# State space stage of a six-stage transformer kernel: its first chunk's normalisation, input projections, gates and step sizes made inside cross attention's last batches

## What is computed

```python
def _L0_attn_ref(u, in_proj_w, dt_projs_weight, dt_projs_bias, x_proj_w, A, D, ...):
    xz = u @ in_proj_w.T
    x, z = jnp.split(xz, 2, axis=-1)
    x = jax.nn.silu(x)
    dt = jax.nn.softplus(x @ dt_projs_weight.T + dt_projs_bias)
    BCp = (x @ x_proj_w.T).reshape(Bsz, L, NHEADS, -1)
    ...
    x_sum = xh.sum(axis=-1)
    zt = Ac[None, None] * (0.5 * dt)[..., None]
    abar = (1.0 + zt) / (1.0 - zt)
    u_in = Bc * ((dt * x_sum)[..., None] / (1.0 - zt))
    # h = abar * h + u_in, step by step; y = Re(C h) summed, times the gate silu(z), projected out

x = x + _L0_xattn_ref(_layernorm(x, axis=-1), ctx_1024, ...)
x = x + _L0_attn_ref(_layernorm(x, axis=-1), ...)
```

## Time and profile before

| what | value |
|---|---|
| median of 3 runs | 1026.29 us (1025.15 to 1029.08) |
| the profiled execution's own time | 1024.24 us |
| its span, first to last instruction | 1022.5 us |
| PE busy | 823.2 us (81%) |
| DVE busy | 746.9 us (73%) |
| ACT busy | 562.1 us (55%) |
| POOL busy | 204.5 us (20%) |
| cross attention | from 0 to 251.1 us of the span |
| state space stage, up to the first step of its recurrence | 252.2 to 299.2 us |

### The profile page before, as it was taken

The page is one execution under the profiler, slowest core; times in us unless marked ns, Lnnn a source line. Parts: engine busy times, 40 slices in busy tenths (PEclk is TensorE's granted clock), DMA queues, the critical chain, the costliest instruction groups (busy, mean ns, idle before and its releaser), DMA issues. The chain is left out here.

```text
span 1022.5 us, 26783 instructions
## 1 busy us (share of the span) xinstructions
PE 823.2 (81%) x9567; PEld 490.9 (48%) x9567; DVE 746.9 (73%) x2473; ACT 562.1 (55%) x1398; POOL 204.5 (20%) x217
## 2 busy tenths in 40 slices
PE   5899999995975788696663397896986999999686
PEld 2577777774322233242131275563664555555343
DVE  5688888884389999999996795456463667767757
ACT  3788898886675658575240476453343333333244
POOL 1467766663000000000000011002210000000136
PEclk9999999998897788898797598997897999999889
DMA  7111111100000000000000903100570000000001
GB/s 241 33 44 43 40 37 41 41 6 2 1 0 0 1 1 0 1 1 0 1 0 8 166 2 117 52 5 19 205 274 1 1 1 0 0 0 1 1 11 31
DMA packets 23157, 36.54 MB, mean 36 GB/s; under 512 B 5668, under 2 KB 19748, under 8 KB 20644
## 3 DMA queue, kind: packets, MB, share of 16 engines
q1 hardware_dynamic: 23080, 35.53, 11.6%
HBM read 34.48 MB, written 1.05 MB: 35 GB/s over the span
## 5 line engine op out<-in xcount | busy, mean ns | idle before, releaser
L381 ACT ACTIVATE xa_prob<-xa_s,xa_nmax 128x257 f32<-128x257 f32 x256 | 128.1, 503 | 21.6 <-DVE xa_nmax L466 19.8
L568 POOL TENSOR_TENSOR xa_prob<-xa_prob,xa_rinv 128x1028 f32<-128x1028 f32 x64 | 121.5, 1900 | 75.8 <-DVE xa_rinv L473 74.6
L466 DVE CUSTOM_DVE_ANT_0 xa_s<-xa_s_ps,xa_nbias 128x257 f32<-128x257 f32 x256 | 93.2, 420 | 12.3 <-ACT xa_prob L381 6.4
L1492 POOL TENSOR_TENSOR mo_disp_t<-mo_disp_t,mo_rst 128x256 f32<-128x256 f32 x16 | 9.9, 616 | 377.0 <-DVE mo_rst L1472 377.0
L2117 PEld LDWEIGHTS ca_z_ps<-ca_xn_t,ca_m_t 128*128 128x128 f32 x512 | 62.0, 198 | 30.5 <-issue 26.0
L2200 ACT COPY ca_z<-ca_z_ps 128x512 f32<-128x512 f32 x64 | 37.5, 585 | 69.0 <-PE ca_z_ps L2117 69.0
L242 PE MATMUL xa_t_ps<-identity,xa_prob 128*128 128x128 f32 x512 | 69.4, 279 | 3.7 <-ACT xa_p_t L390 2.1
L2117 PE MATMUL ca_z_ps<-ca_xn_t,ca_m_t 128*128 128x128 f32 x512 | 67.9, 288 | 4.1 <-ACT ca_xn_t L2194 3.9
L456 DVE COPY xa_kvs<-xa_kv_ps 128x512 f32<-128x512 f32 x64 | 44.1, 689 | 34.5 <-PE xa_kv_ps L216 34.5
L242 PEld LDWEIGHTS xa_t_ps<-identity,xa_prob 128*128 128x128 f32 x512 | 54.8, 141 | 25.3 <-issue 25.3
L390 ACT COPY xa_p_t<-xa_t_ps 128x1024 f32<-128x1024 f32 x64 | 63.4, 990 | 2.7 <-PE xa_t_ps L242 2.7
(11 more groups left out here) (327 smaller groups left out, 1929.1 us busy)
## 6 DMA issues: line engine op xcount, KB each, us to landing
xa_ctx_t<-in_ctx_t SPq DMA_DIRECT2D x64, 128.5 KB, 2.1
room<-in_ctx_t SPq DMA_DIRECT2D x8, 1028.0 KB, 6.6
room<-in_ctx_n SPq DMA_DIRECT2D x8, 1024.0 KB, 4.8
ss_wx<-in_ss_wx SPq DMA_DIRECT2D x1, 2048.0 KB, 7.8
xres<-in_x SPq DMA_DIRECT2D x4, 256.0 KB, 5.5
out_x<-xres SPq DMA_DIRECT2D x4, 256.0 KB, 2.3
ma_mask_u<-in_mask SPq DMA_DIRECT2D x4, 128.5 KB
room<-in_ca_wk SPq DMA_DIRECT2D x1, 512.0 KB, 4.9
```

What stands on the lines that cost most here:

```text
L381: nc.scalar.activation(prob[:, r, g, :], s_sb[:, b, g, :], ACT.Exp, bias=nmax[:, r, g:g + 1], scale=-1.0, accum_out=rsum[:, r, g:g + 1]).t ...
L466: nc.vector.tensor_tensor_reduce(out=s_sb[:, b, g, :], in0=s_ps[:, g, 0:S], in1=nbias[:, g, :], scale=1.0, scalar=3e38, op0=ALU.add, op1=A ...
L568: nc.gpsimd.tensor_tensor(prob[:, r, :, :], prob[:, r, :, :], bc(rinv[:, r, :].rearrange("p (g o) -> p g o", o=1), (P, G, S)), ALU.mult).t ...
```

## The change

Everything of chunk 0 up to `tx` (the product of step size and input sum) moves from the beginning of the state space block into the slots of tiles 14 and 15 of cross attention and the three slots behind them. The tiles and semaphores it needs are made ahead of both stages, in the new class `FirstChunk`. PSUM is borrowed: `kv_ps` for the transpose and the fourth projection, `s_ps[0]` to `s_ps[2]` for the first three, `s_ps[0]` and `s_ps[1]` again for the sums of the step sizes. The statistics of tiles 0 to 3 give `rstd` and `nmr` through Ln and Exp instead of Sqrt and a reciprocal, so cross attention's Exp now comes from the set that has Ln too (L413 before). Silu is loaded between the turns of batches 61 and 62, and the Exp and Ln set again before softplus. The state space block then computes `rstd` and `nmr` of all 16 tiles in the same manner and starts with the projection of B.

```diff
+            def chunk_turn():
+                pe.wait_ge(ch.xn_ready, QT)
+                pe.wait_ge(kv_ready, NT)
+                for i in range(QT):
+                    last = nc.tensor.transpose(kv_ps[:, i * P:i * P + P], ch.xn[:, i, :], ident[:, :])
+                last.then_inc(ch.xnt_mm, 1)
+
+            def chunk_in(parts):
+                pe.wait_ge(ch.xnt_ready, 1)
+                pe.wait_ge(ss_ld, SS_LD)
+                pe.wait_ge(s_ready, G * NT)
+                for j in parts:
+                    nc.tensor.matmul(s_ps[:, j, :] if j < 3 else kv_ps[:, :], ss_in[:, j * P:j * P + P], ch.xnt[:, :],
+                                     start=True, stop=True).then_inc(ch.in_mm, 1)
+
+            def chunk_sizes(part):
+                pe.wait_ge(ch.in_ready, 2)
+                for kb in range(2):
+                    last = nc.tensor.matmul(s_ps[:, part, :], ss_dt[:, part, kb, :], ch.xs[:, 0, kb, :], start=(kb == 0), stop=(kb == 1))
+                last.then_inc(ch.x_mm if part else ch.dt_mm, 1)
+
             def slot(i, j, b):
                 t = i * 2 + j
...
+                if later(t, T - 2) and isinstance(t, int):
+                    if (t, b) == (T - 1, 1):
+                        chunk_turn()
+                    if (t, b) == (T - 1, 2):
+                        chunk_in((0, 1))
+                    if (t, b) == (T - 1, 3):
+                        chunk_in((2, 3))
                 if inside(t, b + 5):
...
+                    if isinstance(t, int) and t == T:
+                        chunk_sizes(0)
                 if b == 2 and later(t):
...
             pairs(pe, slot)
+            chunk_sizes(1)
```

The above is PE's part; ACT's follows:

```diff
+            def chunk_scales():
+                act.wait_ge(mv_ready, QT)
+                act.wait_ge(ch.set_ready, 2)
+                nc.scalar.activation(ch.log_var[:, 0:QT], mv[:, 0:QT, 1], ACT.Ln, bias=ch.eps[:, :]).then_inc(ch.log_ready, 1)
+                act.wait_ge(ch.a_ready, 3)
+                nc.scalar.activation(ch.a_abs[:, :], ch.a_sq[:, :, 0], ACT.Ln).then_inc(ch.a_ready, 1)
+                act.wait_ge(ch.log_ready, 1)
+                nc.scalar.activation(rstd[:, 0:QT], ch.log_var[:, 0:QT], ACT.Exp, scale=-0.5).then_inc(ch.rstd_ready, 1)
+                act.wait_ge(ch.a_ready, 4)
+                nc.scalar.activation(ch.a_abs[:, :], ch.a_abs[:, :], ACT.Exp, scale=0.5).then_inc(ch.a_ready, 1)
+
+            def chunk_rows(tiles):
+                act.wait_ge(ch.nmr_ready, 1)
+                for t in tiles:
+                    nc.scalar.activation(ch.xn[:, t, :], xres[:, t, :], ACT.Identity, bias=nmr[:, t:t + 1], scale=rstd[:, t:t + 1]).then_inc(ch.xn_ready, 1)
+
+            def chunk_turned():
+                act.wait_ge(ch.xnt_mm, 1)
+                nc.scalar.copy(step_major(ch.xnt[:, :]), batch_major(kv_ps[:, :])).then_inc(ch.xnt_ready, 1)
+
+            def chunk_gates(parts):
+                for j in parts:
+                    act.wait_ge(ch.in_mm, j + 1)
+                    nc.scalar.activation((ch.xs if j < 2 else ch.sz)[:, 0, j % 2, :], s_ps[:, j, :] if j < 3 else kv_ps[:, :],
+                                         ACT.Silu).then_inc(ch.in_ready, 1)
+
+            def chunk_softplus():
+                act.wait_ge(ch.dt_mm, 1)
+                nc.scalar.activation(ch.dt[:, :], s_ps[:, 0, :], ACT.Relu, bias=ss_col[:, 0:1]).then_inc(ch.relu_ready, 1)
+                nc.scalar.activation(ch.soft[:, :], s_ps[:, 0, :], ACT.Abs, bias=ss_col[:, 0:1]).then_inc(ch.soft_ready, 1)
+                act.wait_ge(ch.soft_ready, 1)
+                nc.scalar.activation(ch.soft[:, :], ch.soft[:, :], ACT.Exp, scale=-1.0).then_inc(ch.soft_ready, 1)
+                act.wait_ge(ch.soft_ready, 2)
+                nc.scalar.activation(ch.soft[:, :], ch.soft[:, :], ACT.Ln, bias=ch.one[:, :]).then_inc(ch.soft_ready, 1)
+
             def slot(i, j, b):
                 t = i * 2 + j
...
+                if isinstance(t, int) and (t, b) == (T - 2, 1):
+                    chunk_scales()
                 if inside(t, b + 3):
                     exps(*ahead(t, j, b, 3), range(G // 2))
                 if inside(t, b):
                     turn(t, j, b)
                 if inside(t, b + 3):
                     exps(*ahead(t, j, b, 3), range(G // 2, G))
+                if isinstance(t, int):
+                    if (t, b) == (T - 2, 2):
+                        chunk_rows((0, 1))
+                    if (t, b) == (T - 2, 3):
+                        chunk_rows((2,))
+                    if (t, b) == (T - 1, 0):
+                        chunk_rows((3,))
+                    if (t, b) == (T - 1, 1):
+                        chunk_turned()
+                        nc.scalar.preload_act_table(ACT.Silu)
+                    if (t, b) == (T - 1, 2):
+                        chunk_gates((0,))
+                    if (t, b) == (T - 1, 3):
+                        chunk_gates((1, 2, 3))
 
...
+            nc.scalar.preload_act_table_set("natural_log_exp_and_others")
             exps(0, 0, 0)
...
-            nc.scalar.preload_act_table(ACT.Sqrt)
+            nc.scalar.preload_act_table_set("natural_log_exp_and_others")
+            chunk_softplus()
```

DVE's part (`chunk_squares`, `chunk_constants`, `chunk_means` and `chunk_step_size` hold the instructions that stood at L1112 to L1130, L92, L1001 and L1006 before, and a maximum with 1e-37), and what the state space block loses:

```diff
+            def chunk_means():
+                dve.wait_ge(ch.rstd_ready, 1)
+                nc.vector.scalar_tensor_tensor(nmr[:, 0:QT], mv[:, 0:QT, 0], -1.0, rstd[:, 0:QT], ALU.mult, ALU.mult).then_inc(ch.nmr_ready, 1)
...
+            def chunk_step_size():
+                dve.wait_ge(ch.relu_ready, 1)
+                dve.wait_ge(ch.soft_ready, 3)
+                nc.vector.tensor_tensor(ch.dt[:, :], ch.dt[:, :], ch.soft[:, :], ALU.add).then_inc(ch.dt_ready, 1)
+                dve.wait_ge(ch.x_mm, 1)
+                dve.wait_ge(ch.dt_ready, 1)
+                nc.vector.tensor_tensor(ch.tx[:, :], ch.dt[:, :], s_ps[:, 1, :], ALU.mult).then_inc(ch.tx_ready, 1)
...
                 before = later(t)
+                if isinstance(t, int):
+                    if (t, b) == (T - 2, 0):
+                        chunk_squares()
+                    if (t, b) == (T - 2, 2):
+                        chunk_means()
+                    if (t, b) == (T - 1, 1):
+                        chunk_constants()
...
             output_moments(T - 1)
             keep_moments(T - 1)
+            chunk_step_size()
...
-            turn(0)
-            project_in(0)
-            step_sizes(0)
+            pe.wait_ge(ones_ready, 2)
             project_b(0, range(0, 1))
             spread_steps(0)
...
             def next_chunk(c):
-                nc.scalar.preload_act_table(ACT.Silu)
-                gates(c)
-                nc.scalar.preload_act_table_set("natural_log_exp_and_others")
-                softplus(c)
+                if c >= 1:
+                    nc.scalar.preload_act_table(ACT.Silu)
+                    gates(c)
...
 
-            norm.scalar(act)
+            nc.scalar.activation(ch.log_var[:, :], mv[:, :, 1], ACT.Ln, bias=ch.eps[:, :]).then_inc(ch.log_ready, 1)
+            act.wait_ge(ch.log_ready, 2)
+            nc.scalar.activation(rstd[:, :], ch.log_var[:, :], ACT.Exp, scale=-0.5).then_inc(ch.rstd_ready, 1)
             act.wait_ge(w_ld, W_LD)
-            act.wait_ge(a_sum_ready, 1)
-            nc.scalar.activation(a_abs[:, :], a_sq[:, :, 0], ACT.Sqrt).then_inc(a_abs_ready, 1)
-            act.wait_ge(norm.ready, 2)
-            norm_rows(0)
-            act.wait_ge(set_ready, 7)
+            act.wait_ge(ones_ready, 2)
             next_chunk(0)
+            act.wait_ge(ch.nmr_ready, 2)
             norm_rows(1)
             minus_a_i(0, 2)
```

More of the change, by code:

```diff
@@ L412, in _ @@
             roots(3)
-            nc.scalar.preload_act_table(ACT.Exp)
+            nc.scalar.preload_act_table_set("natural_log_exp_and_others")
             exps(0, 0, 0)
@@ L948, in next_chunk @@
             def next_chunk(c):
-                nc.scalar.preload_act_table(ACT.Silu)
-                gates(c)
-                nc.scalar.preload_act_table_set("natural_log_exp_and_others")
-                softplus(c)
+                if c >= 1:
+                    nc.scalar.preload_act_table(ACT.Silu)
+                    gates(c)
+                    nc.scalar.preload_act_table_set("natural_log_exp_and_others")
+                    softplus(c)
                 squares_b(c, 0)
@@ L2507, in program @@
         ss = state_space_weights(Scope(nc, planes), d)
+        chunk = FirstChunk(Scope(nc, planes))
         with ExitStack() as first:
@@ L2515, in program @@
             (ss, ss_loads), (mo, mo_loads) = issue_later(k, "ss", *ss), issue_later(k, "mo", *mo)
-            run(cross_attention, (tables, x_in, w_in, W_IN, id_in, ss_loads + mo_loads))
-        run(state_space, ss)
+            run(cross_attention, (tables, x_in, w_in, W_IN, id_in, ss_loads + mo_loads, ss, chunk))
+        run(state_space, (ss, chunk))
         planes.close()
```

113 lines of the change are left out of this document (65 added, 48 removed).

## The result

| | before | with the change |
|---|---|---|
| median, in runs taken together | 1025.72 us (1023.46 to 1030.11, 10 runs) | 1019.85 us (1015.33 to 1023.13, 10 runs) |
| ratio, with its 95% interval | | 0.9929 (0.9909 to 0.9950) |
| the profiled execution's own time, span | 1024.24, 1022.5 us | 1023.13, 1021.3 us |
| PE, DVE, ACT busy | 823.2, 746.9, 562.1 us | 833.4, 747.3, 561.0 us |

What follows compares the result with a forecast made beforehand. It took chains of short steps with idle engines on both sides of the barrier as the bound; B's projection, starting at 258.5 and taking 5.5, ends at 264.0 against 269.83, so 1026.29 - 5.8 = 1020.5 us, range 1017.0 to 1026.5.

Steps and rivals of the forecast that it cites:

- Tile 14: Cross attention, tile 14: DVE's added squares cost 0.6 us; ACT's small Ln and Exp hide in a wait growing to 1.3.
- The rows: Cross attention: ACT's normalisation of four tiles adds 0.76 us net of waits, so the copy slips about 1.3 us.
- PE's list: Last three slots of cross attention: PE's in-order steps add up and set the tail; last gather slips 4.4 us.
- The end of the block: End of cross attention: after last gather, sums, softplus and two DVE steps end it at 257.2, a 6.1 us slip.
- The rival of a costlier switch: Table loads in cross attention's last slots: each switch costs 1.4 us more; gain 5.1, 1021.2 us, chance 0.04.
- The first projection of B: Behind the barrier: eight matmuls take 5.5 us, within 3.6 to 5.7; spread of the step sizes 5.8 us earlier.
- The first rival: PE's clock stays up over the barrier, so B's projection takes 3.6 us; gain 7.7, 1018.6 us, chance 0.15.
- the clock falls before the sums: End of cross attention: sums of the step sizes take 3.6 us, not 1.8; gain 4.0, 1022.3 us, chance 0.14.
- the slower rival: Cross attention's tail: PE's list runs at half clock, 11.1 us becoming up to 22.2; loss 5.3, 1031.6 us, chance 0.08.
- The end: Whole kernel: 5.8 us off the median of 1026.29 gives 1020.5 us, 0.57% less.
- a start that is x us earlier should make the end x us earlier: State space stage: later chunks follow chunk 0's recurrence, so the whole 5.8 us gain at the start carries through.
- the rival that only 1 us remains: Behind the start: later clock levels or waits eat the gain, some 1 of 5.8 us left; 1025.3 us, chance 0.14.

Runs made afterwards that it cites:

- e7: The change with chunk 0's two z projections and their gates moved back into the state space block; ratio 0.9897 against the kernel before.
- e1: The changed kernel measured and profiled once more, unaltered; median 1020.82 us, ratio 0.9938 against the kernel before.
- e9: e7 with the second table load (Exp and Ln) behind ACT's copy of the last batch instead of ahead of it; ratio 0.9922 against the kernel before.
- e11: e7 measured once more, unaltered; ratio 0.9932 against the kernel before.
- e5: The change plus two unused matrix products behind PE's last sums in cross attention; ratio 0.9917 against the kernel before.
- e2: The kernel before with only cross attention's Exp taken from the table set that also has Ln; ratio 0.9994.
- e8: e7 plus two unused matrix products, as in e5; ratio 0.9900 against the kernel before.
- e3: Only the scales, constants and four normalised rows of chunk 0 made in cross attention, the rest left in the state space block; ratio 0.9964 against the kernel before.
- e6: The kernel before plus two unused matrix products at the start of the state space block, ahead of the transposes; ratio 1.0002.
- e10: e6 measured once more, unaltered; ratio 1.0007 against the kernel before.

## Why the prediction was right

**Tile 14.** DVE's squares were to cost 0.6 us. ACT's wait moved from 227.42 to 229.82, 2.40, of which 1.89 is the entry: 0.51. The wait did not grow to 1.3 us but stayed at 0.72; ACT's four small instructions filled the rest just as foreseen.

**The rows.** The copy of batch 61 was to slip 1.3 us. It went from 240.00 to 242.88, which is 0.99 over the entry.

**PE's list.** The last gather was to slip 4.4 us; it went from 246.29 to 252.30, 4.12 over the entry. That PE and not ACT sets the tail is shown by ACT's waits for it, 1.79 us before its last copy; e7 shows how near ACT was, since with 1.9 us less on PE it took over after 1.0.

**The end of the block.** Predicted slip 6.1 us; 251.07 became 258.68, 5.72 over the entry. Softplus to DVE's start took 2.79 us from 254.40, predicted 2.82. The rival of a costlier switch did not occur: the copy at 245.90 follows its load by 0.01 us, and with 1.4 us more behind the second load softplus could not have started at 254.40, 0.81 us after the load's end.

**The first projection of B.** This is the step that was mis-sized, or rather whose size is not one number: I took 5.5 us with the half clock, within 3.6 to 5.7. It took 3.67 in the profile of the change and 6.61 in e1. That is over my upper bound: 5.9 of the 6.61 us ran at 0.50, while of the 5.74 us from which I took the bound the last 1.5 at least ran at 1.00, as the earlier trace rows say. In e7, e9 and e11, with the same idle time of 3.11 us, it took 5.27, 5.17 and 5.37. So of five profiles with this gap one met the full clock throughout. I had reckoned with a gap of 2.7 us; the second sums were done 0.8 us before the 255.8 of the sum, the block only 0.4 before its 257.2 (both less the entry).

That e1 starts the recurrence 5.8 us early, just the forecast's number, is luck. The forecast's 5.8 was worked out at the spread of the step sizes, which came 5.2 us early in e1: 0.4 us better at the block's end, 1.1 worse in the projection. The other 0.6 came behind it, where the spread of the scales (L908) met a higher clock, 1.48 us in e1 against 2.09 in the change. The first rival's 7.7 is nearly the change's own -8.1, by the step that it named. The rival "the clock falls before the sums" did not occur in this kernel, and the slower rival neither: the clock was at 1.00 from the transposes to the last sum in both profiles.

**The end.** Forecast 1020.5, measured 1019.85 (1020.82 in e1). Did the start carry to the end one for one? Over the twelve kernels the starts have a mean of -5.6 us and the gains by the ratio one of -5.4, with single pairs off by up to 2.3 us; but each pair sets one execution against the mean of others. The profiles tell more. In nine of the twelve the gain at the end of the stage is within 0.4 us of that at the start (e11: 0.7). In the change and e5 it is 2.1 us smaller, in e1 0.8. My step "a start that is x us earlier should make the end x us earlier" failed by this much. The loss lies in one place, where the last chunk is prepared; before, and with the change:

```profile
417.29 7.69 PE L744 MATMUL ss_bank<-ss_xs,ss_wx 128*128 128x512 f32 x16
...
432.49 5.18 PE L711 MATMUL ss_bank<-ss_xnt,ss_win 128*128 128x512 f32 x8 [1.24 <-ACT ss_xnt L864]
```

```profile
410.74 9.36 PE L892 MATMUL ss_bank<-ss_xs,ss_wx 128*128 128x512 f32 x16
...
427.62 6.02 PE L859 MATMUL ss_bank<-ss_xnt,ss_win 128*128 128x512 f32 x8 [0.78 <-ACT ss_xnt L1009]
```

```profile
435.56 0.69 DVE L1230 TENSOR_TENSOR ss_yr<-ss_bank,ss_rms_c 128x512 f32<-128x512 f32 x1 [1.85 <-PE ss_bank L939]
...
440.02 0.75 DVE L1236 SCALAR_TENSOR_TENSOR ss_xs<-ss_bank,ss_col,ss_sz 128x512 f32<-128x512 f32 x1 [1.13 <-PE ss_bank L948]
```

The mean clock over the first group was 0.93 before and 0.76 with the change, and DVE then waits for PE 1.85 and 1.13 us, where before it waited 0.56 once. e1 and e5 show the same (9.15 and 9.36 us for the first group; in e1 1.3 us had been gained ahead of it), the ten others, before among them, 7.7 to 7.8. Why the clock falls longer there in all three profiles of the whole change and in no other is open. So the rival that only 1 us remains is out, but what it named, clock levels that fall in other places, took up to 2 us. That the median comes within 0.7 us of the forecast is thus partly luck: the better clock at the barrier and the loss behind it nearly cancel.

**Why the two profiles differ by 1.1 us and the medians by 5.9.** Counted from its span's start, the change begins the recurrence at 292.93 against 299.17 before, 6.2 us earlier, and loses 5.0 of that behind it, 4.1 of them in one stage. The last stage (routed linear) begins at 957.4 against 962.7, and takes 63.9 us against 59.8. It is the stage's own clock: the busy time of its first 27.3 us, after and before,

```profile
957.40:984.70 27.30, 19.83 (x66) 14.02 (x67) 11.96 (x36) 6.08 (x19) 5.36 (x5) 0.55 0.00 0
```

```profile
962.70:990.00 27.30, 19.84 (x79) 12.58 (x79) 15.18 (x46) 8.88 (x29) 8.61 (x11) 0.75 0.00 1
```

shows PEclk 0.55 after and 0.75 before. Over all thirteen profiles this stage took either 59.5 to 59.9 us (before, e1, e2, e7, e8, e11), with a clock of 0.75 in that stretch, or 63.6 to 64.0 (the change, e3 to e6, e9, e10), with 0.55 to 0.56: the kernel before with two unused products is among the latter, and the changed kernel among both. So what was moved does not decide it, and its 4.1 us are more than half of what the change is worth. The rest of the 5.0 us is the loss of 2.1 in the state space stage, less what the stages between gained.

## What to carry to other kernels

A chain of short steps that opens a stage can be laid into the tail of the stage before, where its engines are idle too; its cost there is read by adding up the in-order list of the engine that gets most of the work, and by asking which engine is next when that list is cut. A matrix product that comes first behind a barrier should be costed with both clocks, as two outcomes with a chance each and not as one number. Where a stage's clock scatters by 4 us, count an edit of a few us from a landmark just ahead of it to one just behind it and to one at the stage's end, and let the median of many runs say only whether it arrives.
